# A fused attention and mixture-of-experts kernel: lambda and bias set-up moved, head products of four tiles on VectorE, and the last second layers in another order

## The reference, cut to what matters

```python
# attention, on layernorm(x)
q, k = rotary(x @ Wq), rotary(x @ Wk)          # per token 16 vectors of 16
v = (x @ Wv).reshape(b, s, H, 2 * D)
attn_c = softmax(q_c @ k_c.T / D**0.25) @ v    # c = 1, 2; [8 x 8] scores of each token
lam = exp(sum(lq1 * lk1)) - exp(sum(lq2 * lk2)) + LAMBDA_INIT
a = attn1 - lam * attn2
a = a * rsqrt(mean(a * a) + EPS) * ln_w + ln_b
x = x + (a * (1 - LAMBDA_INIT)).reshape(b, s, E) @ Wo
# experts, on layernorm(x)
weights, idx = top_k(softmax(xf @ w_gate), 2)  # 8 experts, 1024 places each
h = silu(a_half) * g_half                      # a_half, g_half: exp_x @ c_fc
out = h @ c_proj                               # times its weight, added to x at its token
```

## Time and profile before

| | us |
|---|---|
| three runs, median (lowest to highest) | 696.95 (695.79 to 697.55) |
| the profiled execution | 695.95 |
| its span, first to last instruction | 694.1 |
| TensorE busy (matmul) | 634.8 (91%) |
| VectorE busy | 529.8 (76%) |
| GpSimd busy | 512.1 (74%) |
| ScalarE busy | 487.3 (70%) |

### The profile page before, as it was taken

How to read it: one execution, slowest core, us unless ns; L and a number is a source line. 1 busy time by engine, 2 the same in 40 slices (tenths; PEclk the granted TensorE clock), 3 DMA queues, 4 the chain that set the end, 5 groups by cost and what they waited for, 6 DMA issues and landing times. The chain is left out here.

```text
span 694.1 us, 12873 instructions
## 1 busy us (share of the span) xinstructions
PE 634.8 (91%) x3644; PEld 507.8 (73%) x3644; DVE 529.8 (76%) x1202; ACT 487.3 (70%) x1692; POOL 512.1 (74%) x294
## 2 busy tenths in 40 slices
PE   6889999999999999999999997049999999999990
PEld 3567777777777777777777776048898898889880
DVE  3999999999999999999999997214455456455430
ACT  3568889888988998898899888425455455465440
POOL 4446688898899889889989887734567566676534
PEclk9999999999999999999999999559999999999996
DMA  7991113223222322211201001133565664764434
GB/s 197 346 358 42 32 63 108 64 77 109 82 74 93 106 74 71 92 48 31 63 2 32 31 1 32 32 95 106 78 140 111 132 139 77 160 139 67 69 32 51
DMA packets 57836, 63.43 MB, mean 91 GB/s; under 512 B 7449, under 2 KB 53630, under 8 KB 57776
## 3 DMA queue, kind: packets, MB, share of 16 engines
q1 hardware_dynamic: 42416, 45.66, 20.6%
q0 software_dynamic: 15360, 17.08, 14.2%
HBM read 27.57 MB, written 43.78 MB: 103 GB/s over the span
## 5 line engine op out<-in xcount | busy, mean ns | idle before, releaser
L238 POOL TENSOR_TENSOR v_prod<-w_att,v_sb 128x2048 f32<-128x2048 f32 x62 | 233.0, 3759 | 50.4 <-DVE w_att L1012 47.2
L419 POOL DMA_INDIRECT slot_table<-rows,g_slot x128 | 129.1, 1009 | 32.0 <-issue 30.6
L451 POOL DMA_INDIRECT out_dram<-y_sb,e_tok x64 | 99.6, 1557 | 65.3 <-ACT y_sb L679 50.8
L979 DVE TENSOR_REDUCE bank_s<-qk_prod 128x128 f32<-128x2048 f32 x64 | 146.1, 2282 | 0.0
L972 DVE TENSOR_TENSOR qk_prod<-bank_qk,k_sb 128x2048 f32<-128x2048 f32 x64 | 145.8, 2279 | 0.0
L785 PEld LDWEIGHTS bank_a<-ident,v_prod 128*128 128x128 f32 x1024 | 115.5, 141 | 33.8 <-issue 30.4
L762 PE MATMUL bank_qk<-wqkv,xT 128*128 128x512 f32 x256 | 120.7, 594 | 4.7 <-DVE qk_prod L972 4.7
L785 PE MATMUL bank_a<-ident,v_prod 128*128 128x128 f32 x1024 | 122.3, 273 | 1.0 <-POOL v_prod L238 1.0
L762 PEld LDWEIGHTS bank_qk<-wqkv,xT 128*128 128x128 f32 x256 | 43.7, 190 | 36.2 <-issue 36.2
L773 PE MATMUL bank_v<-wqkv,xT 128*128 128x265 f32 x256 | 69.3, 393 | 0.0
L670 ACT CAST h_hi<-hidden 128x512 fp32r<-128x512 f32 x48 | 29.9, 622 | 55.8 <-DVE hidden L1222 55.8
(11 more groups left out here) (168 smaller groups left out, 1417.5 us busy)
## 6 DMA issues: line engine op xcount, KB each, us to landing
slot_table<-fill SPq DMA_DIRECT2D x8, 1056.0 KB, 13.1
xe<-slot_table SPq DMA_DIRECT2D x16, 528.0 KB, 3.7
out_dram<-x_ring SPq DMA_DIRECT2D x16, 512.0 KB, 3.0
x_ring<-in_L_attn_x_dram SPq DMA_DIRECT2D x15, 512.0 KB, 3.6
w<-in_L_ffn_c_fc_dram SPq DMA_DIRECT2D x8, 768.0 KB, 5.1
w<-in_L_ffn_c_proj_dram SPq DMA_DIRECT2D x8, 384.0 KB, 5.7
slot_table<-rows,g_slot POOLq DMA_INDIRECT x128, 2.5
out_dram<-fill SPq DMA_DIRECT2D x1, 1024.0 KB, 13.5
```

What stands on the lines that cost most here:

```text
L238: eng.tensor_tensor(v_prod[b][:, :, :].rearrange("p m (n e) -> p m n e", n=H), w_att[b][:, :, :].rearrange("p n m -> p m n").unsqueeze(3). ...
L419: pool.indirect_dma_start(out=table, out_offset=bass.IndirectOffsetOnAxis(ap=g_slot[g % SLOT_BUFS][:, j, k:k + 1], axis=0), in_=rows[:, r, ...
L451: pool.indirect_dma_start(out=out, out_offset=bass.IndirectOffsetOnAxis(ap=e_tok[n % 2][:, k:k + 1], axis=0), in_=y_sb[n % 2][:, k, :], in ...
L979: nc.vector.tensor_reduce(scores[b].rearrange("p (c s) -> p s c", c=2), qk_prod[b][:, :].rearrange("p (s c d) -> p s c d", c=2, d=D), AX_X ...
```

## The change

1. `LAST_V` goes from NT - 2 to NT - 4: the head products of tiles 60 and 61 too are on VectorE.
2. `lambda_terms` moves on VectorE from ahead of the first score product to behind `score_sum(0)` and `numbers_of_experts` in step 0; `lambda_exps` on ScalarE from step 2 to step 4.
3. The bias split leaves VectorE. ScalarE copies the row out of PSUM (step 5, behind the copy of xT), GpSimd splits it with seven operations behind its first head product, three of them on one row each (rows 0, 32 and 64 of `bias_parts`, which GpSimd clears at the start). The third part is made in the last copy itself, and the masks aren't needed.
4. The second layer of chunk 14 stands behind the first part of chunk 15's first layer, as in all other steps; that of chunk 15 runs over j on the outside, so that it waits for `h_lo` of each part by itself, and signals its two `y_done` in its last third.

```diff
-        LAST_V = NT - 2
+        LAST_V = NT - 4
...
-        def second_layer_after(m):
-            return NHT - 1 if isinstance(m, int) and m == CHUNKS else 0
...
+            chain(pool.memset(bias_parts[:, :], 0.0))
...
+            def bias_split():
...
+                pool.wait_ge(bias_copied, 1)
+                after(pool.tensor_copy(bias_h[0][:, :], bias_f[:, :]))
+                after(pool.tensor_tensor(bias_r[0][:, :], bias_f[:, :], bias_h[0][:, :], ALU.subtract))
+                after(pool.tensor_copy(bias_h[1][:, :], bias_r[0][:, :]))
+                after(pool.tensor_tensor(bias_r[1][:, :], bias_r[0][:, :], bias_h[1][:, :], ALU.subtract))
+                after(pool.tensor_copy(bias_parts[0:1, :], bias_h[0][0:1, :]))
+                after(pool.tensor_copy(bias_parts[32:33, :], bias_h[1][32:33, :]))
+                pool.tensor_copy(bias_parts[64:65, :], bias_r[1][64:65, :]).then_inc(bias_ready, 1)
+                pool.wait_ge(bias_ready, 1)
...
                 if 0 <= i < LAST_V:
                     head_products(pool, i)
+                if i == 0:
+                    bias_split()
...
+            def copy_bias():
+                act.wait_ge(bias_done, 1)
+                nc.scalar.copy(bias_f[:, :], bank_wo[:, 0:E + AUX]).then_inc(bias_copied, 1)
...
-                if i == 2:
-                    lambda_exps()
                 if i == 3:
                     copy_woT()
                 if i == 4:
+                    lambda_exps()
                     copy_gate()
...
                 if live(i):
                     copy_xT(i)
+                if i == 5:
+                    copy_bias()
...
-                    if j == second_layer_after(m) and chunk_live(m, 2):
+                    if j == 0 and chunk_live(m, 2):
                         scale_output(m - 2, b2)
...
+            def last_second_layer(n, b, wb):
+
+                for j in range(NHT):
+                    past(pe, h_lo_ready, n * NHT + j)
+                    for k in range(CB):
+                        if j == 0 and k % 2 == 0:
+                            past(pe, y_scaled, n * CB + k + 1, CB)
+                        parts = ((h_lo, w2_hi), (h_hi, w2_lo), (h_hi, w2_hi))
+                        for i, (h, w) in enumerate(parts):
+                            last = nc.tensor.matmul(p2_y[k // 2][:, (k % 2) * E:(k % 2 + 1) * E], h[b][:, j, k * P:(k + 1) * P], w[wb][:, j, :],
+                                                    start=(j == 0 and k % 2 == 0 and i == 0), stop=(j == NHT - 1 and i == len(parts) - 1),
+                                                    skip_group_check=True)
+                        if j == NHT - 1 and k % 2 == 1:
+                            last.then_inc(y_done, 1)
...
-                    if j == second_layer_after(m) and chunk_live(m, 2):
-                        past(pe, h_lo_ready, (m - 2) * NHT + NHT - 1)
+                    if j == 0 and chunk_live(m, 2):
                         past(pe, w_lo_ready, expert_of(v, turn, 2) * 2 + 1)
-                        second_layer(m - 2, b2, wb2)
+                        if isinstance(m, int) and m == CHUNKS + 1:
+                            last_second_layer(m - 2, b2, wb2)
+                        else:
+                            past(pe, h_lo_ready, (m - 2) * NHT + NHT - 1)
+                            second_layer(m - 2, b2, wb2)
...
                 if i == 0:
                     centre_weights()
-                    lambda_terms()
...
-                if i == 3:
-                    bias_split()
                 if i == 0:
                     numbers_of_experts()
+                    lambda_terms()
```

More of the change, by code:

```diff
@@ L100, in build_block @@
             bias_f = one("bias_f", [P, E + AUX])
-            bias_h = [one(f"bias_h{j}", [P, E + AUX], BF16) for j in range(3)]
+            bias_h = [one(f"bias_h{j}", [P, E + AUX], BF16) for j in range(2)]
             bias_r = [one(f"bias_r{j}", [P, E + AUX]) for j in range(2)]
-            bias_s = [one(f"bias_s{j}", [P, E + AUX]) for j in range(2)]
             bias_parts = one("bias_parts", [P, E + AUX], BF16)
@@ L187, in build_block @@
             sem(n) for n in "wo_transposed woT_copied gate_folded gate_copied bias_done bias_ready".split())
-        wo_scaled = sem("wo_scaled")
+        wo_scaled, bias_copied = sem("wo_scaled"), sem("bias_copied")
         x_transposed, xT_copied, qk_done, v_done, k_copied, aux_copied, v_copied = (
@@ L405, in _, with after @@
             pool.nop().then_inc(consts, 1)
+            def bias_split():
+                n = 0
+                def after(ins):
+                    nonlocal n
+                    n += 1
+                    ins.then_inc(bias_chain, 1)
+                    pool.wait_ge(bias_chain, n)
+                pool.wait_ge(bias_copied, 1)
[7 more added lines that the diff above has]
+                pool.wait_ge(bias_ready, 1)
             def scatter(t):
@@ L935, in lambda_difference @@
                 dve.wait_ge(lam_chain, 4)
[L937 to L959, removed]
             def numbers_of_experts():
```

## The result

The kernel after takes 700.43 us (median of 15 runs, 698.03 to 701.9), the kernel before 696.94 (15 runs on the same chip, 694.7 to 699.43): ratio 1.0046, interval 1.0034 to 1.0059, which is +3.2 us (2.4 to 4.1). The forecast was 699.7 us, +2.8, and slower. The profiled run of after took 701.9 us with a span of 699.8, 5.7 more than the span of before (694.1). The two profiled runs differ by more than the medians do: that of before was 1.0 under its median, that of after 1.5 over its own. Where this comes from is seen in the start.

What follows compares the result with a forecast made beforehand. TensorE paces attention with VectorE nearly full; the chain then runs through GpSimd's scatters, TensorE and GpSimd's scatter-adds. Terms -1.0 + 0.5 + 4.8 - 1.5 = +2.8 us on the 696.95 median gave 699.75 us, range 697.0 to 702.6.

Steps and rivals of the forecast that it cites:

- The head products: Hand-over: two more products on VectorE delay the slot numbers that GpSimd's scatters wait for, 4.8 us slower.
- The bias split: Start: split moved to GpSimd ahead of product 1, TensorE's restart sooner, gain 1.0 us (2.0 to -0.7).
- B: Start: time of GpSimd's seven bias-split operations, taken as 4.1 us within bounds of 3.1 to 5.8.
- Lambda: Start: VectorE's first score product at 12.1 us, 2.2 sooner, and what follows on VectorE 1.9 us sooner.
- The start's clock: Start: TensorE stands still for 4 us and may fall to 1.2 GHz; loss of 0.5 us (0 to 2.3).
- The tail: Last second layers: rearranged so TensorE, not chunk 14's adds, holds the last adds; gain 1.5 us (2.0 to 0.5).
- the lag: Tail: chunk 15's first GpSimd add starts 1.26 us behind ScalarE's start.
- The sum: Whole kernel: -1.0 + 0.5 + 4.8 - 1.5 = +2.8 us, 699.75 us against the median.
- Rival (b): Hand-over: GpSimd, not the slots, holds the scatters; sum -2.5, 694.4 us, faster; chance 0.08.
- (c): Start: long bias split near 5.8 us and TensorE's clock lost; sum +6.7, 703.6 us; chance 0.12.
- (a): Gains balance: split about 3.1 us, TensorE keeps its clock, tail -1.8; sum +0.7, about 697.7 us; chance 0.25.

Runs made afterwards that it cites:

- e7: The kernel before with the head products of the last six tiles on VectorE (58 and 59 too): 707.18 us, ratio 1.0145.
- e10: The kernel before with only lambda's steps moved behind the first head products, bias split still on VectorE: 696.44 us, ratio 0.999.
- e1: The kernel before with only the head products of tiles 60 and 61 moved to VectorE: 702.53 us, ratio 1.0071.
- e3: The kernel before with only the second layers of chunks 14 and 15 rearranged: 696.33 us, ratio 0.9981.
- e8: The kernel before with only chunk 14's second layer moved ahead, chunk 15's done whole, output by output: 698.13 us, ratio 1.0014.
- e2: The kernel before with only the lambda steps and the bias split moved: 697.84 us, ratio 0.9996.
- e4: The changed kernel with the head products of tiles 60 and 61 back on GpSimd: 696.32 us, ratio 0.999 to the kernel before.
- e5: e4 with the bias split behind GpSimd's product 1 in place of product 0: 691.85 us, ratio 0.9922 to the kernel before.
- e12: e11 plus a GpSimd wait for the first output pair and a small memset ahead of chunk 15's first add: 687.8 us, ratio 0.9869.
- e6: e2 with eight unused 128x512 matmuls on TensorE ahead of sum of heads 1: 698.89 us, ratio 1.0028 to the kernel before.
- e9: e2 with four unused 128x512 matmuls on TensorE ahead of the second sum of the heads: 695.22 us, ratio 0.9978 to the kernel before.
- e11: e5 with 16 unused matmuls on TensorE while it waits for the scatters at the hand-over: 689.41 us, ratio 0.9884 to the kernel before.

## Why the prediction was right, point by point

**The head products: right.** +4.8 forecast, 4.92 between the two traces, +4.9 alone (3.8 to 6.1). The step that carried it (GpSimd is not what the scatters wait for, the slot numbers are queued behind VectorE) is shown by the 12.26 us of idleness, and by e7 with twice as many products.

**The bias split: right in size and place.** B 4.1 forecast, 3.9 measured: two-input operations of 265 columns 0.69 us (0.75 forecast), one-input ones 0.41 (0.4). The interpolation between rows was nearer than the estimate from the page. The Trainium skill (GPSIMD Engine Reference, sections 3.1 and 4.1) led to 2.9 and to 698.5 for the whole. The trace doesn't agree with that estimate, mostly since 265 columns with one input took 0.41 us and not 0.22.

**Lambda: right.** VectorE's first product starts at 12.19 us (12.1 forecast), and e10 moves the restart by 1.74 us (1.9).

**The start's clock: mechanism right, size off, and the sum saved by what it was added to.** The term was 0.5 us. Between the profiled runs it is 2.4 us, more than the 2.3 that bounded it (a bound read from twelve matmuls, while the clock stayed low over more than those). Against the other runs before it is smaller, because that kernel pays too: in the profiled runs of e1, e3, e7 and e8, which have its start, the clock falls at 40.3 to 41.1 us, behind the pause of 3.1 us, for 3.4 us, as here in e3:

```profile
42.21 1.98 PE L808 MATMUL bank_wo<-wo_s,aT_n 128*128 128x265 f32 x4
```

Of 29 runs of the kernel before that were made beside e1, only five have the mean clock of its profiled run, 0.969. What the forecast named as a possibility ("the other runs before may be paying part of it already") is what holds: e2's −0.3 us by the ratio (+0.6 by the medians) stands against −0.5 forecast for the whole start. That 0.5 came near was luck in part: no row told how often either kernel loses the clock.

**The tail: mechanism right, size half.** −1.5 forecast, −0.65 between the traces. The step that failed is the lag: 1.26 us was read at chunk 14, the last chunk has 1.94 (0.68 us); the other 0.2 us is ScalarE's start, 677.23 in the time of before where the forecast had 677.0. Of that 0.08 us is a break ahead of the third part (682.51 to 682.59 in after), and the rest was not taken apart. Before, this lag was hidden, as chunk 15's adds followed those of chunk 14. By the ratio of e3 it is −1.3 (−2.4 to −0.3), which holds both numbers; the traces of after, e3 and e4 agree on 0.65 to 0.67.

**The sum.** Between the profiled runs 1.35 + 4.92 + 0.2 − 0.65 = 5.8, where the spans differ by 5.7; forecast 2.8. By the ratio it is +3.2, by the medians +3.5. So the range held and the side was right, but the profile of before was a run that had kept its clock, and the two traces alone would have shown a loss of 5.7 us. Rival (b) is ruled out by e7; (c) described the profiled run of after nearly (the clock lost, +6.7 against +5.7), though not with a long split; (a) needed the clock kept and a tail of 1.8.

## What to carry to other kernels

Work that is moved to an idle engine goes behind what the pacing engine waits for next there, not ahead of it: the same seven operations, one step later, made the kernel 4.7 us faster (e5 against e4), and TensorE then waited for them and the product behind them for 0 us in e5's trace and 0.8 us in e12's. An engine with much idle time at the end of a phase can be idle because it waits for the full one; moving work from the first to the second then costs its whole length. And where TensorE leaves a pause, look whether the profiled run kept its clock, and what the other runs show, before a difference of 2 us is given to an edit; and look at the whole start, as e5's loss at 26.5 us stands ahead of everything that the edit moved.

## What the hardware did that I had not expected

**VectorE held for the length of a GpSimd operation.** In after, e2, e4, e6 and e9 VectorE's small normalization, 0.28 us in rows 4, took thirteen times that:

```profile
33.61 3.61 DVE L1023 TENSOR_TENSOR p_norm<-probs,p_rec 128x128 f32<-128x128 f32 x1
```

It began 0.27 us behind GpSimd's product 1 (33.34) and ended 0.15 us behind it. The Trainium skill (SBUF — State Buffer, section "Who interferes with whom") says that a VectorE instruction with two SBUF inputs contends with a GpSimd instruction that reads SBUF, that the ports they share are locked by one of them at a time, and that the order of issue decides which of them waits. With that the trace agrees. It was not on the path here: in e4 the restart came at the forecast time in spite of it.

**Scatters beside VectorE's products.** GpSimd's scatter takes 0.97 us, and 2.52 and 2.57 us where it meets one of VectorE's head products, which have two SBUF inputs. Both of these, and the 2.58 of rows 9, end 0.85 or 0.86 us behind the end of the product (409.31 and 427.97 in after, 421.70 before): a scatter that comes while the product runs is held until it is over. The same section infers that such an instruction leaves the generation of GpSimd's DMA descriptors alone. These rows show a scatter held as a whole; whether it is the making of its descriptors that waits, or its reading of the slot numbers, which lie in SBUF, was not told apart.

**A pause doesn't always cost the clock.** The same code with the same pause of 3.7 us kept 2.4 GHz in e4's profiled run and lost it in e2's and after's; e10 lost it at its restart with 1.88 us of waiting just ahead. The wait of 1.92 or 1.93 us for VectorE ahead of the projection near 26 us is in every trace; the profiled runs of e5, e10 and e11 lost the clock behind it (at 26.3 to 27.4 us), the eleven others kept it. Where the clock was lost in the start, it stayed low for 3.4 us (e3) to 6.8 us (e2), and the matmuls in it took up to twice as long.
